# Earlier reciprocals: the softmax denominators' round trip through memory is moved to the head of SyncE's slot and to the end of VectorE's

## The reference, cut

```python
q, k, v = to_heads(q), to_heads(k), to_heads(v)      # 8 heads of 16
attn1 = softmax(q * dh**-0.5 @ k_landmarks^T)        # (b, h, 4096, 64)
out = attn1 @ attn2_inv @ (attn3 @ v)                # ctx = attn2_inv @ (attn3 @ v)
out = out + depthwise_conv(v, conv_w)                # 33 taps along the tokens
t2 = ... x + out @ w_out + b_out                     # and the residuals
wx = layernorm(t2) @ W^T                             # input of the recurrence
```

## Time and profile before

| | |
|---|---|
| three executions | 6308.84, 6314.95, 6308.59 us (median 6308.84) |
| profiled execution: own time, span | 6308.84 us, 6307.2 us |
| PE busy, share of the span | 5771.7 us, 92% |
| ACT, DVE, POOL busy | 3327.7 us (53%), 3073.6 us (49%), 1544.3 us (24%) |
| 116 slots of the output stage, 2825.62 to 3881.94 | 1056.32 us |
| mean granted TensorE clock, whole span | 0.97 |

### The profile page before, as it was taken

One profiled execution on the slowest core, in us unless ns is written; L12 is line 12 of the kernel. 1 busy time (PEld: TensorE's weight loads), 2 busy tenths in 40 slices (PEclk: granted clock), 3 DMA queues, 4 the chain that ended last, 5 costly groups with the idle time before them and its releaser, 6 DMA issues. The chain is left out here.

```text
span 6307.2 us, 245679 instructions
## 1 busy us (share of the span) xinstructions
PE 5771.7 (92%) x103087; PEld 3572.4 (57%) x103376; DVE 3073.6 (49%) x8383; ACT 3327.7 (53%) x9741; POOL 1544.3 (24%) x1997
## 2 busy tenths in 40 slices
PE   5599999998789887989999999899999999999999
PEld 4599888997566665864444444333333333333333
DVE  8677777776777776537877788200000000000000
ACT  5465555565666665338888888233333333333333
POOL 2100000001877774016666666100000000000000
PEclk7799999998999999989999999899999999999999
DMA  8532111123877773037777776211211111211111
GB/s 363 228 109 81 55 54 67 68 82 130 252 228 218 227 230 106 13 104 209 209 211 209 209 211 173 62 44 46 59 46 45 44 46 46 57 46 46 46 44 45
DMA packets 852741, 751.78 MB, mean 119 GB/s; under 512 B 70352, under 2 KB 729808, under 8 KB 848592
## 3 DMA queue, kind: packets, MB, share of 16 engines
q1 hardware_dynamic: 837328, 634.82, 33.8%
q0 software_dynamic: 14336, 101.45, 4.0%
HBM read 425.72 MB, written 308.45 MB: 116 GB/s over the span
## 5 line engine op out<-in xcount | busy, mean ns | idle before, releaser
L2138 PE MATMUL f_junk<-f_idle 128*32 128x384 bf16 x24736 | 1565.9, 323 | 7.0 <-issue 7.0
L2181 ACT ACTIVATE f_y<-f_acc 128x16 f32<-128x16 f32 x4096 | 750.4, 183 | 1556.8 <-PE f_acc L2149 1556.8
L2149 PEld LDWEIGHTS f_acc<-f_y,f_vT 128*32 128x32 f32 x32768 | 649.6, 108 | 1409.2 <-ACT f_y L2181 1397.3
L2149 PE MATMUL f_acc<-f_y,f_vT 128*32 128x16 f32 x32768 | 1049.5, 193 | 58.8 <-issue 9.5
L2096 DVE TENSOR_TENSOR f_sum<-f_turned,f_t 128x512 f32<-128x512 f32 x128 | 88.5, 692 | 1763.0 <-PE f_turned L2131 1762.9
L2138 PEld LDWEIGHTS f_junk<-f_idle 128*32 128x32 bf16 x24736 | 447.7, 96 | 10.8 <-issue 10.5
L1854 DVE TENSOR_REDUCE o_m<-o_bank_l 128x8 f32<-128x512 f32 x512 | 325.6, 678 | 166.4 <-remote 156.6
L422 ACT ACTIVATE l_gate<-l_pf,l_bf 128x256 f32<-128x256 f32 (+12 forms) x768 | 272.6, 406 | 226.6 <-PE l_pf L397 226.3
L388 PE MATMUL l_pf<-l_x,l_wf 128*128 128x256 f32 (+12 forms) x1536 | 317.5, 329 | 36.3 <-DMA l_x<-skew 36.3
L359 POOL DMA_DIRECT2D hidden<-l_h x48 | 36.2, 754 | 1257.6 <-DVE l_hsum L476 1192.6
L941 ACT ACTIVATE a_p<-a_s 128x512 f32<-128x512 f32 x512 | 264.1, 603 | 147.7 <-PE a_s L830 147.7
(11 more groups left out here) (244 smaller groups left out, 12093.8 us busy)
## 6 DMA issues: line engine op xcount, KB each, us to landing
o_v<-vals SPq DMA_DIRECT2D x256, 272.0 KB, 3.4
a_hid<-hidden SPq DMA_DIRECT2D x112, 520.0 KB, 4.7
hidden<-l_h POOLq DMA_DIRECT2D x48, 1040.0 KB, 6.4
skew<-gn_skew POOLq DMA_DIRECT2D x8, 6144.0 KB, 22.9
l_x<-skew SPq DMA_DIRECT2D x48, 1024.0 KB, 5.2
vals<-a_v SPq DMA_DIRECT2D x128, 272.0 KB, 3.2
gn_x<-in_x SPq DMA_DIRECT2D x16, 2048.0 KB, 15.3
a_xin<-in_x SPq DMA_DIRECT2D x128, 256.0 KB, 4.7
```

The source lines that it names most:

```text
L2138: nc.tensor.matmul(junk[rows, :], idle[:, 0:QUAD], idle[:, :], start=True, stop=True)
L2149: mm = nc.tensor.matmul(acc[k % 2][rows, t, :], vT[:, rows], before, start=False, stop=True, skip_group_check=True)
L2181: nc.scalar.activation(y[q][:, u, :], acc[u // RC % 2][:, u % RC, :], ACT.Sigmoid).then_inc(s_y, 1)
```

## The change

On SP `spread(c - 1)` and `broadcast(c - 1)` go to the head of the slot, ahead of the stores and the load of the base, and `pack(c)` goes ahead of the v loads. On VectorE the reciprocals of group c are taken at the end of slot c, where those of group c - 1 were taken in the middle of it. The waits inside the functions stay as they are. `reciprocals(b, c)` waits for the pack of group c.

```diff
             def slot(b, c, q, first, last):
+                if precedes(c, 1, first):
+                    spread(b, c - 1)
+                    broadcast(b, c - 1)
                 if precedes(c, 5, first):
                     store_wx(b, c - 5)
                 if precedes(c, 3, first):
                     store_t2(b, c - 3)
                     if follows(c, 1, last):
                         load_base(*at(b, c + 1))
-                if precedes(c, 1, first):
-                    spread(b, c - 1)
+                pack(b, c)
 
                 if c < GT and b + 1 < B:
                     wait(sp, "conv", NG * (b + 1))
...
                     load_v(b + 2, 0, c - GT)
-                if precedes(c, 1, first):
-                    broadcast(b, c - 1)
-                pack(b, c)
                 if follows(c, 6, last):
...
                 if precedes(c, 1, first):
-                    reciprocals(b, c - 1)
                     merge(b, c - 1)
...
                     statistics(b, c - 5)
+                reciprocals(b, c)
             for k in range(GT):
                 maxima(0, 0, k)
             each_image(dve, slot)
             residual(B - 1, NG - 3)
-            reciprocals(B - 1, NG - 1)
             merge(B - 1, NG - 1)
```

## The result

The changed kernel takes 6413.59 us (median of four runs, 6404.94 to 6418.56), the kernel before beside it 6308.72 us; the ratio is 1.0167 with a 95% interval of [1.0148, 1.0185], so it is slower, by 105 us. The forecast was +66 us, 6375.

A forecast was written before the change was run, and what follows sets the result against it. Output-stage slots of 9.106 us were taken as TensorE's 8.82 us floor plus ScalarE's wait at `even`. A 9.6 us ring would replace this: +57 us over 116 slots, +9 in image 15, 6308.84 + 66 = 6375 us, range 6300 to 6440.

The forecast's parts named there:

- The excess over the floor: Output stage, 116 slots: mean 9.106 us against TensorE's floor of 8.82 us, 33 us in all.
- The wait at `even`: ScalarE's copy to `even` waits for the previous slot's pack DMAs; the change removes it, up to -33 us.
- A ring R, S, B, wx, t2, base, P, R: Per slot: reciprocal (R), spread (S), broadcast (B), stores wx, t2, base load, pack (P), R; sets period at 9.6 us.
- S to B: Ring's second term, on SP: from the spread's issue to the broadcast's issue, 2.55 us.
- B to P landed: Ring's third term: from the broadcast's issue until the pack has landed, 768 KB between, 6.65 us.
- R to S: Ring's first term: from the reciprocal's start on VectorE to the spread's issue on SP, 0.37 us.
- the upper value, 7.25: Upper value for broadcast's issue to pack landed: 4.25 us plus 3.0 us for the three transfers between.
- P's issue: On SP the pack is issued 3.5 us earlier in its slot, at about 3806.9 instead of 3810.42.
- Sum: 116 slots +57 us, seven slots of image 15 +9, all else 0: total +66, 6375 us.
- rival B: Ring of 9.0 to 9.15 us, near today's mean; lost time equals the wait removed, 6298 to 6322 us; 8%.
- Rival A: Ring fits under TensorE's 8.82 us, pack landing 5.9 us or sooner after broadcast's issue: faster, 6276 us; 15%.
- term 3: Ring's time from broadcast's issue to pack landed: 4.25 us with pack straight behind, 6.65 us with the 768 KB between.

The follow-up runs named there:

- e1: Kernel before with two buffers for `even`, so ScalarE's copy waits for the pack of two groups ago: 6271.78 us against 6303.42.
- e4: Changed kernel with SP's order spread, v loads, broadcast, pack, wx, t2, base, xnT: 6278.68 us against 6303.42 for the kernel before.
- e2: Changed kernel with the two stores and the base load put behind the pack on SP: 6402.04 us against 6303.42 for the kernel before.
- e7: Changed kernel with the two pack DMAs issued by ScalarE in its own hardware queue: 6397.12 us against 6305.88 for the kernel before.
- e8: Changed kernel with each 256 KB base load issued a second time into an unread tile: 6524.37 us against 6305.88 for the kernel before.
- e3: Changed kernel with only the v loads put back between spread and broadcast on SP: 6423.15 us against 6303.42 for the kernel before.
- e5: Kernel before with only the reciprocals moved to the end of VectorE's slot, SP's order as before: 6508.3 us against 6305.88.
- e6: Kernel before with only SP's order changed, reciprocals still in the middle of VectorE's slot: 6552.38 us against 6305.88.

## Why the prediction was right

- *The excess over the floor, 33 us.* Right: e1 gives 32, with slots of 8.81 us where 8.82 was read.
- *The wait at `even` goes.* Right, and 33 us are gained there and lost again.
- *A ring R, S, B, wx, t2, base, P, R closes and sets the period.* Right: the four parts of the turn add up to the period, and VectorE's reciprocal waits in all 116 slots, TensorE behind it (1.2 us a slot at L1628, 139.9 / 116, where about 0.8 was expected). Image 15 shows it best: without v loads, and with less work for TensorE, its slots are 9.65 us beside the 9.6 that was forecast. That it is so near is in part luck, for two terms are off in opposite directions there: S to B is 2.38, not 2.55, and B to P landed 7.03, not 6.65.
- *Its size.* R to S: 0.37 forecast, 0.38 found. S to B: 2.55 forecast, 2.53 found. B to P landed: 6.65 forecast, 6.98 found, 7.09 in the turn shown. This is the term that was mis-sized, by 0.33 us a slot; 0.28 remain against the ring as it was rounded, 33 us over the 116 slots. I had taken a value near the lower end, on the ground that the same work only changes places; the upper value, 7.25, was nearer. Of the 0.33, 0.24 lie between the issues: B to P's issue takes 2.34 where 2.1 was reckoned with the issue times of the kernel before, and wx takes 0.46 instead of 0.36 us, t2 in some turns 1.0 instead of 0.4. The v loads are not the reason, since the term is 7.03 in image 15 as well.
- *P's issue.* It was to come 3.5 us earlier in its slot, at 6.5 us. It comes at 8.1 on the mean, 2.1 earlier than before (10.2), since the ring itself keeps SP back.
- *Sum.* 57 + 9 forecast; 90.0 + 9.4 measured in the stretches, and about 8 us elsewhere, unexplained. The times of rival B, 6298 to 6322, are a little wide of its rings: 9.0 to 9.15 us give 6301 to 6320.
- *Rival A.* Refuted here: P landed 7.0 us after B's issue. In e4, where nothing stands between B and P and v fills the wait for S, the faster outcome came about after all. The Trainium skill, DMA: Bandwidth & Descriptors, section "Anatomy of one DMA", fits one transfer as 2.0 us plus its bytes at 436 GB/s, and it does so for DMAs that GpSimd issues, which the prediction did not say; all of the ring's are SyncE's. An estimate from it puts P's landing 4.4 us after B's issue, and the trace of the changed kernel, with 7.0, does not agree.
- *Not seen.* That what goes ahead of S counts as much as what goes ahead of P. By the prediction's terms, P directly behind B should have sufficed (4.25 us instead of 6.65 in term 3, and e2 measures 4.2); e2 shows that S then comes late.

## What to carry to other kernels

Before a round trip through memory is moved earlier, write down the ring that it closes (reciprocal, spread, broadcast, pack and back), with everything that the queue carries in between, and compare its length with the slot: here the pack's deadline moved some 4 us earlier and its issue only 2. A transfer that waits for another to land left the DMA engines nearly empty for about 2.7 us in the turn shown; something independent belongs there, and the small transfer on which engines wait belongs ahead of the large ones that can wait. In this kernel only the two together helped (e4). Where a single-buffered tile makes an engine wait for a DMA, try the second buffer first: it gave at least as much (32 us) as the best new order (25 us; the intervals of e1 and e4 overlap), and it touches nothing else.

## What the runs showed of the hardware that was not expected

- Small DMAs on a queue of their own were not faster: on the mean P took 5.13 us from ScalarE's queue (e7, one execution), 4.64 from SP's behind 768 KB, and 3.48 from SP's directly behind B (e2).
- In a turn one of SP's issues took about 1.0 us where the same issue otherwise took 0.4 to 0.6: the first of P 1.01 in the changed kernel and 0.56 before, the base load 1.07 in e8 and 0.57 in the changed kernel (medians). What sets it stays open.
- The v loads (L1432) put between S and B lengthened the ring by 0.14 us (e3), 256 KB put between B and P by 0.99 (e8). SP had been waiting in the first place, and not in the second.
- TensorE's mean granted clock was 1.00 in the stretch of the changed kernel, 0.97 in those of e5 and e8 and 0.94 in that of e6; below 1.00 the engine was for a part of the stretch at the lower of its two levels, 1.2 instead of 2.4 GHz. TensorE was busy 1030.68 us of 1146.35 in the first and 1040.62 of 1273.93 in the last. In e8 the four parts of the ring, none of them TensorE's, add up to the slot, so the clock is not needed to explain it; how much of e5's and e6's cost it is was not measured. The prediction counted nothing for the clock, and in the changed kernel that held.
